# Column-major tokens and swapped turns in a windowed attention block

## The reference

```python
h = layernorm(x, norm1_g, norm1_b)
hw = h.reshape(B, H // WIN, WIN, W // WIN, WIN, C)
hw = hw.transpose(0, 1, 3, 2, 4, 5).reshape(-1, N, C)      # N = 64 tokens of a window
qkv = (hw @ qkv_w + qkv_b).reshape(Bw, N, 3, HEADS, HD)
...
attn = jnp.einsum('bhnd,bhmd->bhnm', q * SCALE, k)
bias = rel_bias_table[REL_IDX].transpose(2, 0, 1)
attn = jax.nn.softmax(attn + bias[None], axis=-1)
out = jnp.einsum('bhnm,bhmd->bhnd', attn, v)
out = out.transpose(0, 2, 1, 3).reshape(Bw, N, C) @ proj_w + proj_b
...
x = shortcut + out
h2 = layernorm(x, norm2_g, norm2_b)
mlp = jax.nn.gelu(h2 @ fc1_w + fc1_b, approximate=False) @ fc2_w + fc2_b
return x + mlp
```

## Time and profile before

| | |
|---|---|
| median of 3 runs | 1095.75 us (1095.21 to 1095.81) |
| the profiled execution | 1095.25 us, span 1093.5 us |
| TensorE busy | 1039.8 us, 95% of the span |
| VectorE busy | 803.0 us, 73% |
| GpSimd busy | 759.6 us, 69% |
| ScalarE busy | 693.9 us, 63% |
| chain that ended last | TensorE 79%, ScalarE 13%, issue 3% |
| of it tokens_t, line 767 | ScalarE, 5% |
| granted TensorE clock | 0.99 over the span |

### The profile page before, as it was taken

The page is one execution under the profiler, slowest core; times in us unless marked ns, Lnnn a source line. Parts: engine busy times, 40 slices in busy tenths (PEclk is TensorE's granted clock), DMA queues, the critical chain, the costliest instruction groups (busy, mean ns, idle before and its releaser), DMA issues.

```text
span 1093.5 us, 26409 instructions
## 1 busy us (share of the span) xinstructions
PE 1039.8 (95%) x7366; PEld 921.9 (84%) x7366; DVE 803.0 (73%) x2301; ACT 693.9 (63%) x1347; POOL 759.6 (69%) x1174
## 2 busy tenths in 40 slices
PE   1999999999999999999999999998899999999997
PEld 0788888888888888888888888887799999999997
DVE  4677777777777777777777777767577777777773
ACT  1566666667666676666666666664476666766664
POOL 5577666776567765677666676565578888988881
PEclk9999999999999999999999999999799999999999
DMA  1011001010011110111100111000011111111111
GB/s 43 28 34 36 33 29 42 32 37 33 29 39 34 36 35 29 36 36 35 36 29 32 40 34 36 31 15 29 1 37 39 39 43 43 43 43 43 43 39 48
DMA packets 24807, 38.25 MB, mean 35 GB/s; under 512 B 4119, under 2 KB 20698, under 8 KB 24794
## 3 DMA queue, kind: packets, MB, share of 16 engines
q1 hardware_dynamic: 24722, 37.90, 11.0%
q10 hardware_dynamic: 72, 0.20, 0.1%
HBM read 25.50 MB, written 12.58 MB: 35 GB/s over the span
## 4 chain that ended last, share of the span: by engine, by line
PE 79%; ACT 13%; issue 3%; POOL 1%; DVE 1%; DMA 1%; ACTq 1%; SPq 0%; DVEq 0%; POOLq 0%
PE scores_ps L596 16%; PE scores_ps L541 12%; PE mixed_ps L556 11%; PE probs_t_ps L548 6%; PE x_ps L526 6%; PE x_ps L589 6%; ACT tokens_t L767 5%; PE x_ps L529 5%; ACT k_blocks L776 4%; PE x_ps L583 4%; PE x_ps L562 3%; ACT probs L789 3%; PE x_ps L533 3%; PE x_ps L573 3%; PE x_ps L567 3%
## 5 line engine op out<-in xcount | busy, mean ns | idle before, releaser
L464 POOL TENSOR_TENSOR lowered<-biased,row_top 128x384 f32<-128x384 f32 x256 | 212.2, 829 | 247.5 <-DVE row_top L982 245.6
L770 ACT ACTIVATE probs_t<-probs_t_ps 128x384 f32<-128x384 f32 x256 | 126.9, 496 | 256.0 <-PE probs_t_ps L548 254.4
L377 POOL TENSOR_TENSOR rstd<-small,minus_half 128x4 f32<-128x4 f32 (+1 forms) x160 | 242.7, 1528 | 0.0
L556 PEld LDWEIGHTS mixed_ps<-v_blocks,probs_t 128*128 128x128 f32 x1536 | 195.6, 192 | 39.9 <-ACT probs_t L770 21.8
L541 PE MATMUL scores_ps<-k_blocks,q_blocks 96*128 96x192 f32 x1024 | 224.8, 343 | 1.6 <-DVE q_blocks L970 1.6
L556 PE MATMUL mixed_ps<-v_blocks,probs_t 128*128 128x66 f32 x1536 | 206.6, 271 | 4.8 <-ACT probs_t L770 1.7
L978 DVE TENSOR_TENSOR biased<-scores_ps,pos 128x384 f32<-128x384 f32 x256 | 142.7, 557 | 81.4 <-PE scores_ps L541 77.1
L596 PEld LDWEIGHTS scores_ps<-wfc,hidden 128*128 128x128 f32 x1536 | 181.6, 192 | 5.9 <-issue 0.3
L596 PE MATMUL scores_ps<-wfc,hidden 128*128 128x96 f32 x1536 | 180.4, 274 | 0.0
L541 PEld LDWEIGHTS scores_ps<-k_blocks,q_blocks 96*128 96x128 f32 x1024 | 163.2, 193 | 3.7 <-DVE q_blocks L970 2.1
L982 DVE TENSOR_REDUCE row_top<-biased 128x6 f32<-128x384 f32 x256 | 141.6, 553 | 8.9
(11 more groups left out here) (100 smaller groups left out, 1576.6 us busy)
## 6 DMA issues: line engine op xcount, KB each, us to landing
x<-in_x SPq DMA_DIRECT2D x128, 96.0 KB
out<-x SPq DMA_DIRECT2D x128, 96.0 KB
x_in<-in_x SPq DMA_DIRECT2D x244, 48.0 KB
x_second<-in_x SPq DMA_DIRECT2D x8, 48.0 KB
x_in<-in_x ACTq DMA_DIRECT2D x4, 48.0 KB
pos_in<-in_L_conv_rel_bias_table SPq DMA_DIRECT2D x8, 10.6 KB
wproj<-in_L_conv_proj_w SPq DMA_DIRECT2D x6, 3.0 KB
wfc_in<-in_L_conv_fc_w SPq DMA_DIRECT2D x2, 36.0 KB
```

The costliest lines, as they stand in the source:

```text
L377: pool.tensor_tensor(rstd[:, groups], small[:, 7, groups], minus_half[:, groups], ALU.pow).then_inc(step, 1)
L464: pool.tensor_tensor(lowered[:, k % 2, :, :], biased[:, k % 2, :, :], broadcast(row_top[:, k % 2, :], 2, TOK), ALU.subtract).then_inc(lowe ...
L556: mm = pe.matmul(mixed_ps[:, at:at + MIX], probs_t[:, h, :], v_blocks[:, part, u, h, :], start=True, stop=True)
L770: act.activation(probs_t[:, :, :], probs_t_ps[:, 0:HEADS * 128].rearrange("p (h q) -> p h q", h=HEADS), ACT.Copy).then_inc(probs_t_ok, 1)
```

## The change

Two things. The tokens of a window are numbered column by column (j, then i). For this tokens_out writes the columns of a half as runs of 4 x 8 neighbours and reads its bank in runs of 8; heads_out reads runs of 8 and writes as before; the DMAs of the bias take one column pj each, with partitions one table row (15 entries) apart, and the copy that spreads it walks the table the other way. And in slot 3 TensorE turns the tokens of the next batch first and the heads second, each with the waits that it had.

```diff
-        def token_view(tokens, half):
-
-            view = tokens.rearrange("c k (ai j) -> c j (k ai)", j=WIN)
-            return view[:, HALF * half:HALF * half + HALF, :]
-
...
-            for pi in range(WIN):
-
-
-                load(pos_in[WIN * pi:WIN * pi + WIN, :, :], bass.AP(
-                    table.tensor, REL * pi, [[1, WIN], [TABLE, HEADS], [1, REL * (WIN - 1) + WIN]]), table_in)
+            for pj in range(WIN):
+
+
+                load(pos_in[WIN * pj:WIN * pj + WIN, :, :], bass.AP(
+                    table.tensor, pj, [[REL, WIN], [TABLE, HEADS], [1, REL * (WIN - 1) + WIN]]), table_in)
...
                 if k == 3:
-                    if not first:
-                        wait(pe, k_ok, 2 * n + 2)
-                        wait(pe, heads_ok, 4 * n)
-                        turn_heads(x_ps[2], 1)
                     if not last:
                         wait(pe, q_ok, 2 * n + 2)
                         wait(pe, normed_ok, 2 * n + 3)
...
                         wait(pe, heads_t_ok, 2 * n - 1)
                         wait(pe, normed_ok, 2 * n + 4)
                         turn_tokens(1)
+                    if not first:
+                        wait(pe, k_ok, 2 * n + 2)
+                        wait(pe, heads_ok, 4 * n)
+                        turn_heads(x_ps[2], 1)
...
-                      pos_all[:, :, :, :].rearrange("p h i j -> p (h i j)"), start=True, stop=True).then_inc(pos_mm, 1)
+                      pos_all[:, :, :, :].rearrange("p h j i -> p (h j i)"), start=True, stop=True).then_inc(pos_mm, 1)
...
-                source = x_ps[half][0:C2, :].rearrange("c (j t) -> c j t", j=HALF)
-                act.activation(token_view(tokens_t[0:C2, :, :], half), source, ACT.Copy).then_inc(tokens_ok, 1)
+                source = x_ps[half][0:C2, :].rearrange("c (j ka i) -> c ka j i", j=HALF, i=WIN)
+                view = tokens_t[0:C2, :, :].rearrange("c k (a j i) -> c (k a) j i", a=2, j=WIN)
+                act.activation(view[:, :, HALF * half:HALF * half + HALF, :], source, ACT.Copy).then_inc(tokens_ok, 1)
...
-                act.activation(heads_t[0:C2, :, at:at + 2 * WIN * UNITS],
-                               bank[0:C2, :].rearrange("c (ubi j) -> c j ubi", j=WIN), ACT.Copy).then_inc(heads_t_ok, 1)
+                act.activation(heads_t[0:C2, :, at:at + 2 * WIN * UNITS].rearrange("c j (ua i) -> c j ua i", i=WIN),
+                               bank[0:C2, :].rearrange("c (ua j i) -> c j ua i", j=WIN, i=WIN), ACT.Copy
+                               ).then_inc(heads_t_ok, 1)
...
-                                       [REL, WIN], [1, WIN]])
+                                       [1, WIN], [REL, WIN]])
```

## The result

The changed kernel takes 1067.28 us (1065.67 to 1069.46) against 1095.48 for the kernel before. The ratio is 0.9746, with a 95% interval of 0.9727 to 0.9766. That is 28.2 us less, where 26.1 were forecast; the forecast time was 1069.5 us. The profiled execution took 1067.18 us, span 1065.4.

What follows compares the result with a forecast made beforehand. TensorE, busy 22.44 of 22.90 us a batch, plus its hold-ups, bounds the kernel. 29 x (0.31 + 0.58) = 25.8, less 0.3, plus 0.5 and 0.1: 26.1 us less, so 1069.5 us; own range 1067 to 1073, widened to 1066 to 1077.

Steps and rivals of the forecast that it cites:

- Slot 3, 0.31 us: Turning tokens first covers TensorE's wait for k_out before turn_heads; the mix starts 0.31 us earlier in 29 batches.
- The register fetches: Register values the two turns wait on, fetched in TensorE's queue: priced at 0, at most 0.1 us.
- Slot 5, 0.58 us: Faster tokens_out copies, 0.59 us each, remove project_q's wait for them: 0.58 us in each of 29 batches.
- The limit of 1.52 us for the pair: In slot 5 the two tokens_out may last 1.52 us before project_q is delayed; forecast 1.18, so 0.34 to spare.
- The argument that scattered writes and not scattered reads are dear: From tokens_out (1119 ns) against heads_out (588 ns): the scattered SBUF write costs, not the scattered PSUM read.
- What is late next: Slot 3's statistics wait for x_in; idle over 0.90 us delays slot 4's mix: four batches, 0.3 us lost in all.
- rival B: The x_in load keeps the old period's clock and replaces the wait: 1086 us, or 1073 at half the shift; chance 0.10.
- The ends: Outside the 29 regular batches: setup gains 0.5 us, batch 0 0.1, batches 1 and 31 nothing.
- the second phase isn't touched: The phase after the attention batches keeps its steps; no gain was counted there.
- A: tokens_out doesn't get faster; slot 3 still gives 0.31 us a batch, slot 5 nothing: 1086.5 us; chance 0.06.
- C: tokens_out's reads jumping 512 bytes stall ScalarE, making the copy dearer: 1127 us at 1.76 us a copy; chance 0.03.
- D: The edits don't do what they say, undone in the loop by a scheduling effect; chance put at nothing.

Runs made afterwards that it cites:

- e2: The changed kernel with the old token numbering, keeping only slot 3's swapped turns: 1084.32 us, ratio 0.9899 to the kernel before.
- e1: The changed kernel with heads turned first in slot 3 as before, keeping only the new numbering: 1076.32 us, ratio 0.9828 to the kernel before.
- e5: The changed kernel, but the second tokens_out of a pair writes single floats and the first runs of 8: 1071.64 us.
- e3: The changed kernel with the old numbering, tokens_out walking its 4 columns innermost (writes runs of 4 floats): 1067.10 us.
- e6: Against e3, the first tokens_out of a pair writes runs of 2 floats, the second still runs of 4: 1072.06 us.
- e4: The changed kernel unaltered, run again beside other kernels: 1068.16 us, ratio 0.9754 to the kernel before.
- e10: The changed kernel unaltered, run again in another set: 1066.60 us, ratio 0.9745 to the kernel before.
- e9: The changed kernel with batch 31's GpSimd sums earlier, its root in four parts, and batch 0's other_weights in two steps: 1060.58 us.

## Why the prediction was right, point by point

**Slot 3, 0.31 us.** Right: 1.96 became 1.64, and e2 shows it alone. The register fetches cost nothing that shows.

**Slot 5, 0.58 us.** Right in size and in its cause: 1.77 became 1.19, and e1 shows it alone. The new copy is 585 ns, where 0.59 was forecast. The limit of 1.52 us for the pair was tested by e5 at 1.53 and holds within 0.01. The pair itself was 0.12 us shorter than forecast, since I added two durations where the second copy overlaps the first. It lay inside the slack. The argument that scattered writes and not scattered reads are dear was drawn from two rows, and e3 and e6 bear it out.

**What is late next.** Right in its mechanism. The path from the load to slot 4's mix is 1.92 us again. In batch 23 the load was latest, statistics after 1.14 us of idle time:

```profile
550.72 0.98 DVE L889 BATCH_NORM_STATS2 stats<-x_in 128x6 f32<-128x48 f32 x8 [1.14 <-DMA x_in<-in_x]
```

```profile
552.64 0.88 PE L551 MATMUL mixed_ps<-v_blocks,probs_t 128*128 128x66 f32 x6
```

550.72 + 1.92 = 552.64, where the mix starts, 0.26 later than it would. Over the execution the statistics waited 18.4 us in 29 batches, as before the change, and 17.4 and 11.4 us in e4 and e10: the load kept its distance to slot 3, and rival B (a load tied to the old clock) is out. The idle times crossed 0.90 in batches 18 and 23; I had counted four such batches for 0.3 us. In all, batches 2 to 30 took 639.12 - 29 x 22.02 = 0.54 us more than 29 undisturbed periods. The period itself fell by 0.91 us (22.93 to 22.02), not by 0.89. The two small errors go against each other, and batches 2 to 30 together came out 25.77 us shorter, where 25.8 less 0.3 was forecast.

**The ends.** Here the misses are. Setup: 0.5 was forecast and 0.74 found. In the stretch around the copy it is 0.49: from the start of the second turn to project_q 2.35 us passed (22.81 to 25.16) and now 1.86 (22.56 to 24.42). The other 0.25 is the first load, which came 0.27 earlier; that is chance. Batch 0: from the first project_q to slot 6's mix 26.48 us before and 26.30 after, so 0.18, where I took 0.1. Nothing hangs on this difference: the same distance is 27.15 us in e4 and 24.93 in e10. The wait there is now for VectorE and has grown to 1.29 us, as the term implied: what slot 5 gave went into this wait. The first line is that mix, the second the mix in slot 4 of batch 1:

```profile
50.72 0.85 PE L551 MATMUL mixed_ps<-v_blocks,probs_t 128*128 128x66 f32 x6 [1.29 <-DVE heads L989]
```

```profile
67.76 0.88 PE L551 MATMUL mixed_ps<-v_blocks,probs_t 128*128 128x66 f32 x6 [0.78 <-DVE heads L989]
```

Batch 1 gained 0.3 us where I took 0, because its load came 0.3 us sooner after the step that issues it; the wait of the earlier trace rows is still there.

**What no term had.** Behind batch 30 another 0.66 + 0.45 = 1.1 us went, where the forecast has nothing, since "the second phase isn't touched". That step stands. In e4 and e10, the same program, batch 31 and the change of phase took 51.58 and 51.47 us and the second phase 306.4 and 306.3, as in the kernel before (51.56 and 306.3). The steps are the same, and the difference is the speed at which TensorE ran them: a product of the first layer takes 0.79 us in the kernel before (773.25 on) and 0.50 at the same place in the changed one (746.20 on), since the clock had risen again. The stretch from the first turn of normed2 to the first product of the second layer is 24.22 us before and 23.62 in the changed kernel, and 22.37 to 24.31 in the other kernels whose lines don't differ there. So this part of the 28.2 us is no gain of the change. Without it and the load's 0.25 the profiled execution shows 26.7 us. The three sets of the changed kernel came out 28.2, 26.8 and 28.3 us below the kernel before beside them. The forecast of 26.1 holds for what the edits do, and the time of the first set lies 2.2 us under the 1069.5, near the low end of the range, by chance in the stages around the loop.

**Rivals.** A (the copy stays slow) would have shown tokens_out above 760 ns; it is 585. B is out by the load's distance. C is out by the same 585 ns, and by e3: even single floats read 512 bytes apart cost nothing. D: e1 and e2 show each edit doing what it says.

## What to carry to other kernels

On an engine that is always busy, look for holes between starts, not for idle time: compare a stretch with the same instructions elsewhere, and add what each hole is worth times how often it comes. When a wait is to be covered by other work of the same slot, work out by how much the producer may be late, since only what lies beyond that counts. A copy that changes a layout should have its scattered side where it is cheap: here four floats in a row on the writing side were enough, got by turning the order of two loops, and no renumbering was needed.

## What the runs showed of the hardware

- ScalarE's fp32 copy of 96x512 from PSUM to SBUF: 1119 ns when single floats are written 32 bytes apart (1052 in the other order of e5), 621 with runs of 2, 581 to 585 with runs of 4, 8 or 32. Reading single floats 32 or 512 bytes apart costs nothing that shows (588 and 581 to 585 ns, against 581 for a bank read straight through in e5). Only the size of the step from 1 to 2 was new to me.
- Two such copies in a row start 0.48 us apart when fast and 0.88 apart when slow (means over the kernel), where the first of them lasts 0.58 and 1.09 us. So 0.1 and 0.2 us of the first lie under the second.
- TensorE's granted clock fell to its lower level (0.50) for some 10 us after a wait of 1.29 us in one profiled execution of e6, and stayed at 1.00 after the same wait in the changed kernel. It cost e6 some 5 us (batches 0 and 1 in 50.36 us, where the other profiles with that wait took 43.06 to 45.54). Executions of one program differ by 1.0 us (e4) to 5.2 us (e3). With fewer long waits e9's executions lie within 1.8 us; that the waits are the cause of the spread fits these runs, but it wasn't tested apart.
